# Softmax rows scaled on ScalarE and the adjacency term added, transposed, on VectorE as the probabilities leave PSUM

## What is computed

```python
    def _L2_gnn_ref(x, mask, adjacency_mat, distance_mat, W_qkv, W_out, b_out):
        ...
        dots = jnp.einsum('bhid,bhjd->bhij', q, k) * scale
        m2 = mask[:, None, :, None] & mask[:, None, None, :]
        dots = jnp.where(m2, dots, -big)
        attn = jax.nn.softmax(dots, axis=-1) * LA
        adj = jnp.where(m2, adjacency_mat[:, None], 0.0)
        dist = jnp.where(m2, distance_mat[:, None], big)
        attn = attn + LG * adj + LD * jnp.exp(-dist)
        out = jnp.einsum('bhij,bhjd->bhid', attn, v)
        ...
    x = _layernorm(x + _L0_gnn_ref(x, adj, L0_gnn_W), axis=-1)
    x = _layernorm(x + _L1_gnn_ref(x, adj, ...), axis=-1)
    x = _layernorm(x + _L2_gnn_ref(x, nodemask, adj, adj, ...), axis=-1)
    x = _layernorm(x + _L3_gnn_ref(x, adj, ...), axis=-1)
```

## Time and profile before

| what | value |
|---|---|
| median of 3 runs | 1298.9 us (1297.4 to 1299.2) |
| the profiled execution | 1298.51 us, its span 1296.7 us |
| PE busy | 1272.6 us, 98% of the span |
| DVE busy | 1194.8 us, 92% |
| ACT busy | 910.6 us, 70% |
| PE busy, 400 to 600 us | 199.00 of 200 us, granted clock 1.00 |
| DVE busy, 400 to 600 us | 187.98 of 200 us |
| ACT busy, 400 to 600 us | 142.59 of 200 us |

### The profile page before, as it was taken

How to read it: one execution, slowest core, us unless ns; L and a number is a source line. 1 busy time by engine, 2 the same in 40 slices (tenths; PEclk the granted TensorE clock), 3 DMA queues, 4 the chain that set the end, 5 groups by cost and what they waited for, 6 DMA issues and landing times.

```text
span 1296.7 us, 30200 instructions
## 1 busy us (share of the span) xinstructions
PE 1272.6 (98%) x10848; PEld 1162.8 (90%) x10848; DVE 1194.8 (92%) x3789; ACT 910.6 (70%) x2445; POOL 140.7 (11%) x265
## 2 busy tenths in 40 slices
PE   7999999999999999999999999999999999999997
PEld 6899999999898999898999999998989998989986
DVE  6988999999999999999999999999999999999996
ACT  7677767677667677667677676776676776776773
POOL 0100111101111101111101111011111011110011
PEclk9999999999999999999999999999999999999999
DMA  6110111110111110111100111101111101110000
GB/s 227 34 35 2 35 43 43 43 43 3 42 43 43 43 42 2 43 43 43 43 24 20 43 43 43 43 3 43 43 43 43 32 12 43 43 43 9 10 10 25
DMA packets 34306, 49.00 MB, mean 38 GB/s; under 512 B 7920, under 2 KB 16880, under 8 KB 34160
## 3 DMA queue, kind: packets, MB, share of 16 engines
q1 hardware_dynamic: 34160, 47.08, 11.6%
HBM read 38.68 MB, written 8.39 MB: 36 GB/s over the span
## 4 chain that ended last, share of the span: by engine, by line
PE 75%; DVE 17%; issue 4%; ACT 2%; DMA 1%; POOL 0%; SPq 0%; DVEq 0%; POOLq 0%
PE psum L1485 57%; PE psum L1499 6%; PE psum L1735 5%; PE psum L1693 5%; DVE x L901 3%; DVE work L1030 3%; DVE x_pre L959 2%; DVE bn L867 2%; DVE x_pre L1114 2%; DVE x_pre L969 1%; DVE qkT_l L838 1%; DVE x2T_l L838 1%; PE psum L1786 1%; ACT self_part L385 1%; PE psum L1789 1%
## 5 line engine op out<-in xcount | busy, mean ns | idle before, releaser
L534 ACT ACTIVATE work<-work,shift 128x256 f32<-128x256 f32 x512 | 253.6, 498 | 37.8 <-DVE shift L1030 37.8
L1049 DVE SCALAR_TENSOR_TENSOR work<-work,rsum,extra 128x256 f32<-128x256 f32 x512 | 216.6, 474 | 0.1
L1030 DVE CUSTOM_DVE_ANT_0 work<-psum,minus_big 128x256 f32<-128x256 f32 x512 | 189.3, 415 | 1.9 <-PE psum L1693 1.9
L385 ACT ACTIVATE work<-psum 128x512 f32<-128x512 f32 x256 | 138.1, 595 | 73.5 <-PE psum L1499 69.6
L385 ACT ACTIVATE sup_h<-psum 128x512 fp32r<-128x512 f32 x124 | 73.3, 591 | 144.4 <-PE psum L1485 144.2
L342 POOL TENSOR_TENSOR mv<-mv,eps 128x2 f32<-128x2 f32 x128 | 33.3, 260 | 1141.9 <-DVE mv L888 1141.9
L1485 PE MATMUL psum<-x2T_h,wqkv_h 128*128 128x256 f32 x512 | 146.4, 286 | 5.7 <-DVE x2T_l L838 5.5
L1485 PE MATMUL psum<-x2T_l,wqkv_h 128*128 128x256 f32 x512 | 143.1, 279 | 0.0
L1485 PE MATMUL psum<-x2T_h,wqkv_l 128*128 128x256 f32 x512 | 143.1, 279 | 0.0
L1499 PE MATMUL psum<-ident,work 128*128 128x128 f32 x1024 | 129.0, 274 | 0.0
L1735 PE MATMUL psum<-work,v_sb 128*64 128x256 f32 x1024 | 124.6, 385 | 0.0
(11 more groups left out here) (182 smaller groups left out, 3720.1 us busy)
## 6 DMA issues: line engine op xcount, KB each, us to landing
xT_sb<-in_xT SPq DMA_DIRECT2D x32, 256.0 KB, 2.7
adjT_sb<-in_adjT SPq DMA_DIRECT2D x32, 256.0 KB, 3.0
adj_sb<-in_adj SPq DMA_DIRECT2D x32, 256.0 KB, 4.6
x_sb<-in_x SPq DMA_DIRECT2D x32, 256.0 KB, 4.8
out<-y_sb SPq DMA_DIRECT2D x32, 256.0 KB, 4.5
work<-in_wqkv SPq DMA_DIRECT2D x1, 1536.0 KB, 10.6
mask_row<-in_nodemask SPq DMA_DIRECT2D x32, 32.0 KB, 4.5
w_raw<-in_w SPq DMA_DIRECT2D x3, 256.0 KB, 6.1
```

Source lines behind the costliest of these rows:

```text
L385: return nc.scalar.activation(dst, src, ACT.Copy, scale=scale)
L534: last = nc.scalar.activation(prob[:, p % 2, i, h], prob[:, p % 2, i, h], ACT.Exp, bias=shift[:, p % 2, h, i:i + 1], scale=-1.0, accum_out ...
L1030: last = V_.tensor_tensor_reduce(out=prob[:, p % 2, i, h], in0=bank(SCORES[p] + h)[:, i * N:(i + 1) * N], in1=minus_big[:, g % 2, i], scal ...
L1049: last = V_.scalar_tensor_tensor(out=prob[:, p % 2, i, h], in0=prob[:, p % 2, i, h], scalar=rsum[:, p % 2, h, i:i + 1], in1=extra[:, g % 2 ...
```

## The change

- The adjacency term is made from the transposed adjacency (`adjT_sb`), so `extra` is transposed too.
- DVE `probs` is gone. ACT gets `probs(g, p)` instead: prob = prob * rsum in place, four instructions of 128x256 for a pair, whose scale is a column of `rsum`.
- ACT `probs_t` is gone. DVE gets `probs_t(g, p, h)` instead: probT = transposed probabilities from PSUM + `extra`, one instruction of 128x512 for a head.
- PE's steps and their order stay; where it waited for `dve_prob` it waits for `act_prob`, where for `act_probT` for `dve_probT`. SP's queue and POOL's stay as they are.
- The orders of ACT and DVE are written anew around this. Also `adj_exp` moves behind `probs(g, 1)`, `adj_sum` to the end of DVE's slot and `adj_extra` to the next slot.

```diff
             def adj_exp(g):
-                act.wait_ge(dma_adj[g % 2], loaded(g))
+                act.wait_ge(dma_adjT[g % 2], loaded(g))
                 reuse(act, dve_extra, once(g - 1))
-                nc.scalar.activation(exp_adj[:, :, :], adj_sb[:, g % 2], ACT.Exp, scale=-1.0) \
+                nc.scalar.activation(exp_adj[:, :, :], adjT_sb[:, g % 2], ACT.Exp, scale=-1.0) \
                     .then_inc(act_exp_adj, 1)
...
-            def probs_t(g, p, h):
-                act.wait_ge(pe_probT, nth2(g, p, h))
-                copy(probT[:, p % 2, h], halves(bank(PROBT[p][h]))).then_inc(act_probT, 1)
+            def probs(g, p):
+                act.wait_ge(dve_rsum, nth(g, p))
+                for h in range(2):
+                    for i in range(NT):
+                        last = copy(prob[:, p % 2, i, h], prob[:, p % 2, i, h], scale=rsum[:, p % 2, h, i:i + 1])
+                    last.then_inc(act_prob, 1)
...
-            def probs(g, p, h):
-                if h == 0:
-                    dve.wait_ge(dve_rsum, nth(g, p))
-                for i in range(NT):
-                    last = V_.scalar_tensor_tensor(out=prob[:, p % 2, i, h], in0=prob[:, p % 2, i, h],
-                                                   scalar=rsum[:, p % 2, h, i:i + 1], in1=extra[:, g % 2, i],
-                                                   op0=ALU.mult, op1=ALU.add)
-                last.then_inc(dve_prob, 1)
+            def probs_t(g, p, h):
+                dve.wait_ge(pe_probT, nth2(g, p, h))
+                if p == 0 and h == 0:
+                    dve.wait_ge(dve_extra, once(g))
+                V_.tensor_tensor(probT[:, p % 2, h], halves(bank(PROBT[p][h])), extra[:, g % 2], ALU.add) \
+                    .then_inc(dve_probT, 1)
...
                 values(s - 2)
+                probs(s - 2, 1)
+                adj_exp(s)
                 self_copy(s)
...
             def slot(s):
+                probs_t(s - 5, 2, 0)
+                probs_t(s - 5, 2, 1)
+                probs_t(s - 5, 3, 0)
+                probs_t(s - 5, 3, 1)
+                hidden_lo(0, s - 3)
                 scores(s - 4, 0, 0)
-                hidden_lo(0, s - 3)
```

More of the change, by code:

```diff
@@ L594, in slot @@
                 hidden_hi(1, s - 1)
-                adj_exp(s)
                 exps(s - 2, 1, 1)
+                probs(s - 2, 0)
                 mask_bias(s - 1)
@@ L618, in slot @@
                 sup_hi(0, s)
+                probs(s - 2, 2)
                 tail_qkv(s - 3)
                 out_hi(s - 2, 1)
+                probs(s - 2, 3)
                 qk_hi(s - 1, 1)
@@ L672, in first_graphs @@
                 exps(0, 1, 1)
+                probs(0, 0)
+                probs(0, 1)
                 qk_hi(0, 2)
@@ L691, in first_graphs @@
                 exps(0, 3, 1)
+                probs(0, 2)
+                probs(0, 3)
                 qk_hi(1, 0)
                 qk_hi(1, 1)
-                probs_t(0, 2, 0)
-                probs_t(0, 2, 1)
-                probs_t(0, 3, 0)
                 hidden(0, 2)
-                probs_t(0, 3, 1)
                 hidden_hi(0, 2)
@@ L715, in first_graphs @@
                 exps(1, 1, 1)
+                probs(1, 0)
+                probs(1, 1)
                 self_copy(3)
@@ L734, in first_graphs @@
                 qk_hi(2, 0)
+                probs(1, 2)
+                probs(1, 3)
                 tail_qkv(0)
@@ L754, in first_graphs @@
                 qk_hi(2, 2)
+                probs(2, 0)
                 hidden(1, 3)
                 hidden_hi(1, 3)
+                probs(2, 1)
                 self_copy(4)
@@ L778, in first_graphs @@
                 exps(2, 3, 1)
+                probs(2, 2)
+                probs(2, 3)
                 sup_hi(0, 4)
@@ L807, in last_graphs @@
                 exps(G - 1, 3, 1)
+                probs(G - 1, 2)
+                probs(G - 1, 3)
                 tail_qkv(G - 2)
@@ L928, in adj_sum @@
                 dve.wait_ge(act_exp_adj, once(g))
[L929 removed]
+                V_.tensor_tensor(exp_adj[:, :, :], exp_adj[:, :, :], adjT_sb[:, g % 2], ALU.add) \
                     .then_inc(dve_adj_sum, 1)
@@ L1132, in slot @@
                 recip_sums(s - 4, 0)
+                adj_extra(s - 3)
                 qk_lo(s - 4, 2)
-                probs(s - 4, 0, 0)
-                probs(s - 4, 0, 1)
                 degrees(s - 2)
                 hidden_lo(1, s - 3)
-                adj_sum(s - 2)
                 recip_sums(s - 4, 1)
                 norm_apply(3, s - 7)
-                probs(s - 4, 1, 0)
                 attention_out(s - 5)
@@ L1145, in slot @@
                 norm_stats(2, s - 5)
-                probs(s - 4, 1, 1)
                 gcn_out(s - 3)
@@ L1183, in slot @@
                 tail_gate(s - 5)
-                adj_extra(s - 2)
             def first_graphs():
@@ L1248, in first_graphs @@
                 recip_sums(0, 1)
-                probs(0, 0, 0)
-                probs(0, 0, 1)
                 qk_lo(0, 2)
@@ L1258, in first_graphs @@
                 norm_apply(0, 2)
-                probs(0, 1, 0)
-                probs(0, 1, 1)
                 gcn_out(1)
@@ L1264, in first_graphs @@
                 norm_mean(1, 1)
+                probs_t(0, 0, 0)
+                probs_t(0, 0, 1)
+                probs_t(0, 1, 0)
+                probs_t(0, 1, 1)
                 scores(0, 2, 0)
@@ L1283, in first_graphs @@
                 out_lo(0, 1)
-                adj_extra(2)
             def last_graphs():
+                probs_t(G - 4, 2, 0)
+                probs_t(G - 4, 2, 1)
+                probs_t(G - 4, 3, 0)
+                probs_t(G - 4, 3, 1)
                 scores(G - 3, 0, 0)
@@ L1298, in last_graphs @@
                 recip_sums(G - 3, 0)
+                adj_extra(G - 2)
                 x1_bias(G - 2)
-                probs(G - 3, 0, 0)
                 hidden_lo(1, G - 2)
@@ L1305, in last_graphs @@
                 gate_probs(G - 5)
-                probs(G - 3, 0, 1)
-                probs(G - 3, 1, 0)
-                probs(G - 3, 1, 1)
                 adj_lo(G - 1)
@@ L1342, in last_graphs @@
                 tail_k(G - 4)
-                probs(G - 3, 2, 0)
-                probs(G - 3, 2, 1)
-                probs(G - 3, 3, 0)
-                probs(G - 3, 3, 1)
                 norm_mean(3, G - 5)
@@ L1363, in last_graphs @@
                 out_lo(G - 3, 3)
-                probs(G - 2, 0, 0)
-                probs(G - 2, 0, 1)
                 qk_lo(G - 2, 2)
@@ L1372, in last_graphs @@
                 sup_lo(2, G - 1)
-                probs(G - 2, 1, 0)
                 norm_mean(2, G - 3)
                 gcn_out(G - 1)
-                probs(G - 2, 1, 1)
                 norm_stats(1, G - 1)
@@ L1412, in last_graphs @@
                 out_lo(G - 2, 3)
-                probs(G - 1, 0, 0)
-                probs(G - 1, 0, 1)
                 recip_sums(G - 1, 1)
@@ L1417, in last_graphs @@
                 gate_probs(G - 3)
-                probs(G - 1, 1, 0)
-                probs(G - 1, 1, 1)
                 qk_lo(G - 1, 3)
```

117 lines of the change are left out of this document (48 added, 69 removed).

## The result

The changed kernel takes 1516.1 us (median of 4 runs, 1512.3 to 1519.7), the kernel before 1299.05 (1297.4 to 1299.6): a ratio of 1.167, with a 95% interval of 1.164 to 1.171. It is slower, by 217 us, where 188 were forecast and the range reached to 226.

What follows compares the result with a forecast made beforehand. PE was taken to set the time, sharing an edge with DVE at x2T_l; 4.50 + 1.59 = 6.09 us a graph gave 158 us for 26 graphs, plus 30 for six others: 188 on 1298.5, so 1487 us, range 1447 to 1525.

Steps and rivals of the forecast that it cites:

- The first half: From gcn_out to x2T_l: 2.10 us from ACT's queue plus 2.40 from four DVE additions, 4.50 us a graph.
- the second: Second half of the slot: scores(g + 1, 0) waits for DVE's additions and starts 1.59 us late a graph.
- The rival that ScalarE's part is hidden: Scalings and adj_exp cost nothing, only the first half's four additions count: 77 us, 1375 us; chance 4%.
- The rival "not slower": DVE's relief of 1.6 us a graph decides; PE gives only some 5 us, so 1294; chance 2%.
- PE was to be held some 0.7 us at `tail_adj_k`: Second half: tail_k's cast comes 1.40 late, holding PE some 0.7 us, inside the 1.59 of scores.
- DVE was to wait about 1.5 us for qkT_h: Second half: qk_lo(g + 1, 1) waits for ACT, spending what DVE saved; about 1.5 us a slot.
- scalings of 0.31: ACT scalings at 0.31 us start to start instead of 0.40: some 50 us less; low end 1447.
- the term for the other graphs: Six graphs outside the regular order, with additions and scalings in blocks: 30 us, regular price 37, hidden 0.
- scalings at 0.50: High end, ACT scalings without overlap: 0.4 and 0.8 us more a graph, 7.3 x 26 + 37, so 1525.
- The rival that the clock falls: PE's stalls lower its clock in the slots: another 10 us a graph, about 1780 or 1630; chance 5%.
- My sign for being wrong: Wrong if granted clock leaves 1.00 in slots, period is under 43 or over 48 us, or aggregate doesn't wait for ACT.
- The busy shares: Over the span: PE 86% or so, DVE under 80%, ACT near 67% at about 1000 us busy.

Runs made afterwards that it cites:

- the first two experiments: Changed kernel with self_copy ahead of probs(g, 1) and adj_exp, 1464.5 us; changed kernel with tail_qkv, out_hi and qk_hi(g + 1, 1) moved earlier on ACT, 1478.8 us.
- the twin additions: Kernel before plus one unused 128x512 DVE addition per graph: ahead of qk_lo(g, 3), 1316.3 us; ahead of x1_bias, in a gap, 1298.2 us.
- the constant scale: Changed kernel with the 512 scalings' scale a constant instead of a column of rsum: 1477.5 us, ratio 1.138.
- the third: Changed kernel with self_copy moved ahead in ACT's first half and tail_qkv, out_hi and qk_hi ahead in its second: 1424.1 us, ratio 1.096.
- the fourth kernel: Changed kernel with both halves of ACT's slot reordered, and the same moves in ACT's written-out start (graphs 0 to 2): 1409.1 us, ratio 1.085.
- the filled wait: Changed kernel with 24 dummy transposes on PE in the last slot only, where it waits 3.6 us for DVE's addition: 1514.8 us, ratio 1.167.
- the last experiment: On the fourth kernel with adj_exp behind qk_hi(g, 3) and gate_column, DVE's four first-half additions put directly one behind the other: 1425.3 us, ratio 1.099.
- the last two experiments: The fourth kernel with adj_exp behind qk_hi(g, 3) and gate_column, 1405.7 us; then also DVE's four first-half additions together, 1425.3 us.

## Why the prediction was right

The mechanism and its size in the slots held to a few hundredths. The first half was given 4.50 us and measures 4.49, the second 1.59 and 1.62, 26 slots 158 us and 158.7. The parts were tried apart: ScalarE's queue in the first half 1.82 us (2.1 with `adj_exp` moved too, which took the wait for qkT_h), in the second 1.37. The 2.6 left are put down to the additions, which were doubled but never taken out. The rival that ScalarE's part is hidden falls with the first two experiments. The rival "not slower" named the point on which it would turn, idle time between `gcn_out` and x2T_l; the twin additions show both sides of it, 18.6 us inside and 0.6 us, within the noise, in the gap.

Two of the smaller steps were wrong and cost nothing in the sum. In the second half PE was to be held some 0.7 us at `tail_adj_k`, by `tail_k`. It is held one step sooner, at `hidden(0)`, by the bank of `tail_qkv`, and is 1.1 us late there (724.27 is 661.25 in the times of before, with the 4.49 of the first half off, against 660.15 before). That lies inside the 1.62 of `scores`. And DVE was to wait about 1.5 us for qkT_h: it waits 0.7 us for it, after 1.6 us for qkv. The aside that scalings of 0.31 would take some 50 us off the sum doesn't fit the prediction's own low end, which is 40 under the forecast; the constant scale took off 38.6.

The step that was mis-sized is the term for the other graphs, **30 us, taken at most as the regular 37**. It measures 61.6 us (3.4 + 27.2 + 31.0), and the 31.6 that it lacked are as much as the profiled execution takes over the forecast (1518.7 against 1487). That 1516 still lies in the range is luck in part: the upper end had its room from scalings at 0.50, which measured 0.40, and not from this term. "Nothing there is looser than in the slots" was right, but the other side wasn't thought through: in these orders scalings and additions stand in blocks, so PE waits 4.0 us at the start behind eight scalings, and 3.6 us at the end for the first of four additions that stand together behind other steps, where a slot's longest wait is 1.7. ScalarE's order at the start was 16.5 of them (138.4 to 121.9 us for graphs 0 to 3 between the third and the fourth kernel). The end was not reordered. For its 31 us the waits and the clock are seen in the trace, and 4.0 us of it go when one wait is filled. How the rest divides stays open.

The rival that the clock falls was partly true, at another place and price. It costs nothing in the change's slots. The slot from 202.05 to 247.49 us has a stretch at 0.85, and its `attend` shows no wait:

```profile
210.00:220.00 10.00, 9.50 (x75) 8.01 (x74) 9.96 (x36) 5.80 (x20) 0.89 (x2) 0.85 0.00 0
```

```profile
213.08 1.95 PE L1716 MATMUL psum<-work,v_sb 128*64 128x256 f32 x16
```

It starts 11.03 us after v_sb, against 10.89 in the slot at 702.63, where it waited 1.29 us for DVE. The slower products ahead of it only fill the time in which PE would wait, and the slot takes 45.44 us. Every third slot from graph 3 to 27 is like this, nine in all, which is why `attend` counts 17 waits in 26 slots. In the twelve slots whose clock I read, 6 us around `attend` show 0.82 or 0.83 in those and 1.00 in the others. With the additions of the second half doubled, slots at 0.93 and slots at 1.00 (25 us from 5 us behind v_sb) take the same 46.7 us too; only two at 0.86 take more, 47.4 and 47.7. My sign for being wrong, a clock off 1.00 in the slots, came (0.98 and 0.99 over 200 us) and meant nothing by itself. It does cost at the end (the filled wait) and in the last experiment, and, as far as can be told, at the start and with the additions of the first half doubled.

The busy shares: PE 88% where 86 were forecast. In the slots its waits grew by 4.8 us and its busy time by 1.3 (40.5 us a slot against 39.2), which makes the 6.1. Nine slots at the lower clock are over a third of that growth (41.3 us busy in each instead of 40.0); the rest I read as waits that part matmuls which overlapped before (it wasn't tried). DVE 77%, under 80 as said, though its busy time fell by 34 us and not by the 51 of the prediction's relief (1.6 x 32). ACT 975.5 us and 64% where about 1000 and 67% were forecast, which I read as scalings in a row overlapping more than I had taken.

## What to carry to other kernels

Where one engine sets the time, look for the stretches of another engine's queue that run without idle time from a result of the first to a wait of the first: there each added instruction costs about its own length, and in a gap wider than itself the same instruction was free (0.6 us in a gap of 0.8). Moving work between engines is judged by what it puts into such a stretch, not by the busy totals, and on an in-order queue the results that the bounding engine waits for go ahead of everything that is merely ready. After each repair, look for the wait that takes over.

## What the runs showed of the hardware that was not expected

Waits that keep TensorE's total idle time but move it can change its clock. In the last two experiments the waits have the same lengths (0.4, 1.3 and 0.6 us a slot), yet the granted clock stays at 1.00 in the slots of one and falls in 14 of 26 in the other, which is 20 us slower. So the length of the longest wait doesn't decide by itself. The Trainium skill ("TensorE: Matmul & The Clock Gate", section "Part 1: The HAM clock gate (the "warmup" mystery)") says that the clock follows how busy the engine has been; the filled wait agrees (0.71 to 1.00), and why the one pattern is spared and the other not stays open here.
